# Two multi-head attentions on one core: the reads of the query stacks and the maximum rows are issued from ScalarE's queue instead of SyncE's

## The reference

```python
x = L0_attn_x                                    # (16, 256, 128)
# layer 0, attention
q = (x @ Wq.T + bq).reshape(b, s, 16, 8)         # k, v alike
w = jnp.einsum('bshd,bzhd->bhsz', q, k) / jnp.sqrt(8.)
w = jax.nn.softmax(w, axis=-1)
vw = jnp.einsum('bhsz,bzhd->bshd', w, v).reshape(b, s, 128)
x = _layernorm(x + (vw @ Wo.T + bo))
# ... experts, one-head attention, a gated feed-forward ...
# layer 2, attention: the same with a causal mask, no biases
x = _layernorm(x + _L2_attn_ref(x, ...))
```

## Time and profile before

| | us |
|---|---|
| median of 3 runs | 1626.0 |
| lowest and highest | 1621.2 to 1633.96 |
| the profiled execution | 1636.59 |
| its span, first to last instruction | 1634.8 |
| TensorE busy | 1164.4 (71%) |
| VectorE busy | 954.8 (58%) |
| ScalarE busy | 613.6 (38%) |
| GpSimd busy | 498.9 (31%) |

### The profile page before, as it was taken

How to read it: one execution, slowest core, us unless ns; L and a number is a source line. 1 busy time by engine, 2 the same in 40 slices (tenths; PEclk the granted TensorE clock), 3 DMA queues, 4 the chain that set the end, 5 groups by cost and what they waited for, 6 DMA issues and landing times.

```text
span 1634.8 us, 32039 instructions
## 1 busy us (share of the span) xinstructions
PE 1164.4 (71%) x9203; PEld 836.9 (51%) x9203; DVE 954.8 (58%) x3446; ACT 613.6 (38%) x1352; POOL 498.9 (31%) x711
## 2 busy tenths in 40 slices
PE   1498897889468888466644888989887698428840
PEld 1255554555257777355532666767655476326520
DVE  3476886786512222797753565667647688752227
ACT  1165554556233333234510454555555332103210
POOL 5111333433524444332451011111103211443553
PEclk9697887889689999798766899999997799559975
DMA  4223333230245556411103222222101000133422
GB/s 127 71 73 72 80 87 80 77 81 29 93 139 171 159 169 209 151 51 36 33 13 86 61 67 69 67 66 64 38 24 34 23 27 13 43 102 102 127 71 87
DMA packets 120631, 129.59 MB, mean 79 GB/s; under 512 B 14274, under 2 KB 104131, under 8 KB 117315
## 3 DMA queue, kind: packets, MB, share of 16 engines
q1 hardware_dynamic: 112834, 113.75, 24.7%
q0 software_dynamic: 7680, 14.37, 2.5%
HBM read 72.42 MB, written 36.00 MB: 66 GB/s over the span
## 4 chain that ended last, share of the span: by engine, by line
PE 36%; DVE 18%; issue 16%; DMA 14%; POOL 6%; SPq 4%; ACT 3%; another core or an unknown queue 2%; DVEq 1%; POOLq 0%; ACTq 0%
PE po L439 6%; DMA we<-in_pack 4%; DMA xr<-xg 4%; PE po L1492 3%; DVE xg L335 3%; PE pt L399 2%; PE pt L402 2%; PE pt L1486 2%; DMA xs<-xg 2%; POOL rstd L328 2%; PE pm L420 2%; PE pm L1486 2%; DMA scr<-parts 2%; PE pm L426 2%
## 5 line engine op out<-in xcount | busy, mean ns | idle before, releaser
L608 DVE TENSOR_REDUCE mx<-pm 128x2 f32<-128x512 f32 (+1 forms) x512 | 307.1, 620 | 243.7 <-PE pm L426 136.7
L561 ACT ACTIVATE ex<-pt 128x512 f32<-128x512 f32 (+1 forms) x512 | 271.5, 544 | 265.9 <-PE pt L399 132.9
L325 POOL TENSOR_SCALAR ve<-mv 128x2 f32<-128x2 f32 x96 | 25.5, 266 | 601.4 <-DVE mv L319 601.4
L1565 POOL DMA_INDIRECT result<-ye,to_row x144 | 135.7, 942 | 190.8 <-issue 147.2
L439 PE MATMUL po<-ex,va 128*32 128x256 f32 (+1 forms) x2048 | 163.9, 395 | 4.5 <-ACT ob L570 3.6
L402 PE MATMUL pt<-hide_k,ident 128*128 128x128 bf16 x512 | 97.7, 229 | 37.4 <-issue 28.4
L399 PE MATMUL pt<-qs,ks 99*128 99x256 bf16 x512 | 112.0, 307 | 14.9 <-DMA qs<-mt 10.8
L420 PE MATMUL pm<-ks,qs 96*128 96x256 bf16 x512 | 115.7, 313 | 6.3 <-DVE mx L608 5.5
L1492 PE MATMUL po<-he,we 128*128 128x256 f32 (+1 forms) x448 | 113.3, 396 | 5.8 <-DVE yt L1532 4.0
L304 PE MATMUL p<-ident,xs 128*128 128x128 f32 x112 | 40.1, 358 | 99.1 <-DMA xs<-xg 83.5
L309 ACT COPY xt<-p 128x256 f32<-128x256 f32 x112 | 41.8, 373 | 182.9 <-PE p L305 163.0
(11 more groups left out here) (281 smaller groups left out, 2808.8 us busy)
## 6 DMA issues: line engine op xcount, KB each, us to landing
we<-in_pack SPq DMA_DIRECT2D x40, 514.5 KB
xs<-xg SPq DMA_DIRECT2D x112, 128.0 KB
scr<-parts SPq DMA_DIRECT2D x32, 384.0 KB
we<-in_pack SPq DMA_DIRECT2D x16, 512.0 KB
qs<-scr SPq DMA_DIRECT2D x32, 192.0 KB
ks<-scr SPq DMA_DIRECT2D x32, 192.0 KB
yr<-result SPq DMA_DIRECT2D x48, 128.0 KB, 2.2
xe<-sorted SPq DMA_DIRECT2D x40, 132.0 KB
```

What stands on the lines that cost most here:

```text
L561: nc.scalar.activation(ex[j % 2][:, 2 * u:2 * u + 2, lo:S], pt[:, u, :].rearrange("p (b k) -> p b k", k=S)[:, :, lo:S], ACT.Exp).then_inc( ...
L608: nc.vector.tensor_reduce(mx[q.slot % 2][:, qt, 4 * b + 2 * u:4 * b + 2 * u + 2], pm[:, u, :].rearrange("p (b k) -> p b k", k=S)[:, :, 0:h ...
L1565: pool.indirect_dma_start(out=rows, out_offset=bass.IndirectOffsetOnAxis(ap=to_row[q.slot][0:m, i:i + 1], axis=0), in_=ye[q.slot][0:m, i, ...
```

## The change

The reads of the query stack (three for each sequence) and the two transfers of the maximum rows leave SyncE's queue. ScalarE issues the maximum rows right after its own copy to `mt`, at j = 1. It issues the query reads at j = 6, after the exponentials of that j, for the sequence at(1), with the waits that SyncE had for them. The write to `scr` and the key reads stay with SyncE, in the old order. Bytes, sizes and destinations of all transfers stay the same.

```diff
--- before.py
+++ after.py
@@ heads_sync
                 if (q := at(0)):
                     load_x(sp, q, g, n)
-                if (q := at(4)):
-
-                    sp.wait_ge(mt_sb, a + q.n + 1)
-                    for t in range(2):
-                        sp.dma_start(qs[q.slot][MAX_AT:MAX_AT + 3, :, t * P:t * P + P],
-                                     mt[q.slot % 2][STACK * t:STACK * t + STACK, :]).then_inc(mrows[q.slot], 16)
                 if (q := at(1)):
...
                     for first, n_rows in ((0, 24), (24, 16), (40, 8)):
-                        src = scr[q.slot, 0:n_rows // DH, 0].rearrange("t (d h) k -> t d (h k)", h=HEADS)
-                        sp.dma_start(qs[q.slot][first:first + n_rows, :, :].rearrange("r h k -> r (h k)"), src).then_inc(stacked[q.slot], 16)
                         src = scr[q.slot, 3 - n_rows // DH, 1].rearrange("(d h) k -> d (h k)", h=HEADS)
@@ heads_scalar
                         nc.scalar.copy(mt[q.slot % 2][:, :], p0[0:96, S:2 * S].bitcast(BF16)[:, 0:P]
                                        ).then_inc(mt_sb, 1)
+                        wait_apart(act, mt_sb, a + q.n + 1, passed)
+                        for t in range(2):
+                            nc.scalar.dma_start(qs[q.slot][MAX_AT:MAX_AT + 3, :, t * P:t * P + P],
+                                                mt[q.slot % 2][STACK * t:STACK * t + STACK, :]
+                                                ).then_inc(mrows[q.slot], 16)
...
+                    if j == 6 and (q := at(1)):
+                        wait_apart(act, to_scr, 16 * (a + q.n + 1), passed)
+                        wait_apart(act, ts_ps, 16 * (a + q.back(3)), passed)
+                        wait_apart(act, stack_zero, SLOTS * (2 if a == 0 else 3), passed)
+                        for first, n_rows in ((0, 24), (24, 16), (40, 8)):
+                            src = scr[q.slot, 0:n_rows // DH, 0].rearrange("t (d h) k -> t d (h k)", h=HEADS)
+                            nc.scalar.dma_start(qs[q.slot][first:first + n_rows, :, :].rearrange("r h k -> r (h k)"), src
+                                                ).then_inc(stacked[q.slot], 16)
```

## The result

The changed kernel takes 1816.4 us (median; 1812.6 to 1822.6) against 1626.8 us of the kernel before on the same chip. The ratio is 1.117, with a 95% interval of 1.114 to 1.121: 190 us more. The forecast was 1785 us, with a range of 1690 to 1850.

A forecast was written before the change was run, and what follows sets the result against it. TensorE's waits for `xr` and the maximum rows, behind SyncE's stack reads, were read as the bound. New step 12.9 + 1.8 + 13.0 = 27.7 us; +66 and +93 us on the 1626.0 us median gave 1785 us, range 1690 to 1850.

The forecast's parts named there:

- the term that decides: Both attentions: query reads go out a full step later than before, so TensorE stands at j = 1 each step.
- 5.27 us are left: Second attention: time from ScalarE's end of j = 6 to TensorE's next j = 1; 4.75 us in the first.
- The landing: Query reads from ScalarE's issue to last arrival: 9.0 us alone, 14.3 us sharing engines with key reads, 13.0 us taken.
- The clock: TensorE's lower clock after a wait lengthens j = 1 to j = 6 by 1.8 us, bounds nothing and 3.0 us.
- The sum: Step of 27.7 us in both attentions, 13 steps each: 66 + 93 = +159 us on the median, 1785 us.
- The maximum rows: Issued by ScalarE at j = 1, they land at R + 6.1 us (R: TensorE's j = 1), removing 1.9 us a step.
- ScalarE's own time: Issuing on ScalarE: about 2.1 us for query reads with waits, 1.54 us for maximum rows, costed at nothing.
- the cover: TensorE standing at j = 1 anyway hides ScalarE's issuing; without that, 0.9 x 26 = 23 us.
- my 0.9 us: What TensorE would feel a step from ScalarE's issuing, at the copy its next transposition waits for, if not hidden.
- SyncE: Loses its wait for the maximum rows (211.7 us) but then stands for the split parts: nothing gained, nothing lost.
- B: Rival: the two queues do not hinder each other, landing 9.0 us, step 23.7 us, +55 us, 1681 us; chance 0.24.
- C: Rival: reads land inside the 5.27 us, waits fall away, 90 us less, 1536 us or 1559 us; chance 0.06.

The follow-up runs named there:

- e2_q_only: Changed kernel with the maximum rows back on SyncE, so only the query reads move to ScalarE at j = 6: 1808.1 us, ratio 1.114.
- e1_mt_only: Kernel before with only the maximum rows issued by ScalarE after its copy, all six stack reads staying on SyncE: 1637.0 us, ratio 1.008.
- e4_q_j1: Changed kernel with ScalarE's query reads issued at j = 1, behind the maximum rows, instead of j = 6: 1608.5 us, ratio 0.989.
- e9_q_j4: Changed kernel with ScalarE's query reads issued at j = 4 instead of j = 6: ratio 0.9995 to the kernel before.
- e3_no_keys: Changed kernel with the three key reads left out, scores not the reference's: 1640.1 us, ratio 1.009.
- e14_rows: Changed kernel without key reads, query scratch rows contiguous, query reads in 8-row pieces, neighbouring in the first attention, spread in the second: 1558.6 us, run once.

## Why the prediction was right

**What bounds, and the term that decides.** Right. The step from "5.27 us are left" to "TensorE will stand at j = 1 in each step" held in the traces, and `e2_q_only` put nearly the whole loss there. One reading was off without harm: the wait for the maximum rows before was 13.6 us and not 17.3, or 1.5 us a step instead of 1.9. The sum goes by the paces and does not use it.

**The landing.** I took 13.0 out of 9.0 (alone) and 14.3 (shared); measured 14.2 at the step read, and in the mean of twelve steps 14.2 in the first attention and 14.9 in the second, the shared end. The time that I granted to issuing in parallel did not come: the two engines had work for all that time anyway. The lower bound was good too, 8.8 with the key reads left out. Taking the shared bound itself, as the two saturated engines of the earlier trace rows said, would have been right.

**The clock.** I took 1.8 us from a wait of 2.86 us. At the step read, after a wait of 8.6 us, the way from j = 1 to the end of j = 6 was 15.4 - 12.87 = 2.5 us longer than unhindered, within the 0 to 3.0 given. The granted clock was at its lower level until about 1175 us, some 5 us after TensorE had gone on. That way also holds ScalarE's two issues of the maximum rows, but `e2_q_only`, which has them on SyncE, has the same length: 14.8 us to the issue in the mean of both. I had 12.9 + 1.8 = 14.7, so only 0.1 us was missing here in the second attention and 0.4 in the first (15.1).

**The sum.** 27.7 us a step was forecast, 29.2 and 29.7 came: 1.5 and 2.0 us more, nearly all of it landing. Over 12 steps of each attention that is 42 us. I had counted 13 steps: between the fourteenth and the fifteenth sequence, where no key reads come along any more, the step was 21 us again. One step too many in each attention takes 12 of the 42 off. The paces that I subtracted, over 13 and 11 steps, were a little slow: for the twelve steps that count it was 22.5 and 20.3 us, which adds 4. The 4 us that the changed kernel gained between the attentions take as much off. So 30 us are left, the distance from 1785 to 1816. That it is no more is in part luck, since a landing taken too short and a step too many pull opposite ways.

**The maximum rows: right outcome, wrong reason.** I said that on a queue with nothing ahead of them they would land 4 us after the copy. In the changed kernel they land 3.0 us after the first of their two issues and TensorE no longer waits for them in steady steps, but because no stack read is under way at j = 1 any longer. `e1_mt_only` shows the move itself to be worth nothing (+0.8%): from an empty queue they took 8 us at the step read and came when the stack reads were through. Had the forecast been asked for this half alone, it would have been 2.6% off, on the wrong side.

**ScalarE's own time.** The prices were right (1.91 and 1.54 us, on SyncE 1.84 and 1.54), and so was the cover. Where the cover was taken away, 2.2 us a step appeared in `e4_q_j1`, with five issues in one piece. In `e9_q_j4`, with three issues at j = 4 and two at j = 1, TensorE waits 1.8 us a step for ScalarE's copy to `ob` in the second attention. No run shows my 0.9 us, and these two say that it was too low.

**SyncE.** As said: without its wait for the maximum rows it stands for the split parts instead, 611 us in all where the earlier trace rows has 193.9, and its reads go out no earlier.

**The rivals.** B (queues that don't hinder each other) falls with `e3_no_keys`: they do, by 5.6 us. C would have needed a landing under 5 us; even with the better layout it was 7.9, and 5.4 us without any key reads beside it. The Trainium skill ("DMA: Bandwidth & Descriptors", Issuing engines are not separate DMA queues) says that DMAs started on several engines run on the same 16 engines and interleave, so that only issue time is saved. The traces agree: the query reads take 14.2 us beside the other queue's key reads and 8.6 us without them, and all six from one queue take 15.7 us.

## What to carry to other kernels

Moving a transfer to another engine's queue moves it in time, to where that engine's program stands. Count how long before its reader it now goes out, and compare that with the landing beside what is in flight there, before counting the issues that it saves. Here the DMA share stood at two sixteenths while everything waited, and the shape of the transfers was at fault and not their queue: changing the layout gave 6.6%, where every choice of queue and place gave 1.1% at best.

## What the runs showed of the hardware that was not expected

- A small transfer (24 KB) from an otherwise empty queue took 8 us beside reads from another queue on two engines, and arrived when those were through. A second queue gave it no way past.
- Cutting reads in pieces of 8 neighbouring rows raised the DMA share from two engines' worth to nine, at 9 GB/s each instead of 25. The landing fell only from 14.2 to 12.0 us. The Trainium skill ("SBUF — State Buffer", Door 1: The DMA port swizzle) says that groups of four neighbouring partitions share a port. By that, 8 neighbouring rows would reach two ports, an estimate. `e14_rows` (7.4 us with neighbouring rows, 6.4 with spread ones) points the same way and does not settle it.
- In `e14_rows` six pieces with their rows in every third or second place (the last with neighbouring ones) took 3.8 us to issue, 0.6 to 0.7 us for a spread piece. Six pieces of neighbouring rows took 2.0 us, 0.3 us each.
